# A counting sort's step on VectorE: the late count read in the middle of the next step

## What is computed

```python
x = _layernorm(x + _L0_gnn_ref(x, src, dst, edge_type_8, ...))          # gated recurrent update
x = _layernorm(x + _L1_gnn_ref(x, edge_attr_16, We, be, bias, src, dst, 12500))
x = _layernorm(x + _L2_gnn_ref(x, W1, root1, b1, W2, root2, b2, edge_index, edge_type_8))
x = _layernorm(x + _L3_gnn_ref(x, edge_index, W1, b1, W2, b2))
```

## Time and profile before

| | |
|---|---|
| median of 3 runs | 16680.38 us (16605.38 to 16702.47) |
| span of the profiled execution, first to last instruction | 16996.1 us |
| PE busy | 11995.3 us (71%) |
| DVE busy | 10824.2 us (64%) |
| ACT busy | 8088.7 us (48%) |
| POOL busy | 5158.9 us (30%) |
| mean granted TensorE clock | 0.791 |

### The profile page before, as it was taken

The page is one execution under the profiler, slowest core; times in us unless marked ns, Lnnn a source line. Parts: engine busy times, 40 slices in busy tenths (PEclk is TensorE's granted clock), DMA queues, the critical chain, the costliest instruction groups (busy, mean ns, idle before and its releaser), DMA issues. The chain is left out here.

```text
span 16996.1 us, 429738 instructions
## 1 busy us (share of the span) xinstructions
PE 11995.3 (71%) x146289; PEld 8312.1 (49%) x146290; DVE 10824.2 (64%) x19718; ACT 8088.7 (48%) x16130; POOL 5158.9 (30%) x4771
## 2 busy tenths in 40 slices
PE   1343443434434344799799998997996999999998
PEld 0111111111111111466688886665664888888887
DVE  3233333333333333688788887887886899999998
ACT  1232433433424234566466664665664555555554
POOL 1656666565664656000111111000000111111111
PEclk8555555555555555899899998999998999999999
DMA  7122222222222222688222222887885222333322
GB/s 208 48 72 59 81 67 66 81 59 71 74 58 79 58 72 82 184 229 229 89 106 106 106 106 95 234 235 198 235 235 126 80 83 83 85 85 84 84 84 71
DMA packets 1721891, 1905.31 MB, mean 112 GB/s; under 512 B 981549, under 2 KB 1429103, under 8 KB 1696207
## 3 DMA queue, kind: packets, MB, share of 16 engines
q1 hardware_dynamic: 1602775, 1863.79, 37.0%
q0 software_dynamic: 116864, 39.75, 1.5%
q10 hardware_dynamic: 2078, 0.15, 0.0%
HBM read 1449.57 MB, written 453.42 MB: 112 GB/s over the span
## 5 line engine op out<-in xcount | busy, mean ns | idle before, releaser
L688 POOL DMA_INDIRECT rec<-sort_ring,sort_idx x3520 | 4042.6, 1148 | 2791.9 <-issue 1469.7
L1381 DVE TENSOR_TENSOR e_full<-e_feats,e_masks 128x3840 bf16<-128x3840 bf16 x1179 | 2523.7, 2154 | 350.5 <-ACT e_feats L1339 302.0
L1294 PE MATMUL e_acc<-e_full,e_sel 128*128 128x384 bf16 (+1 forms) x11760 | 2120.9, 327 | 270.4 <-DVE e_full L1381 270.2
L778 PE MATMUL sort_ps_count<-sort_hot,upper_b 128*128 x400 | 231.6, 579 | 2689.9 <-DVE sort_hot L903 2144.6
L1530 PE MATMUL e_acc<-e_outer,e_sel 128*128 128x272 f32 x7840 | 1896.8, 397 | 3.9 <-DVE e_outer L1625 3.9
L1337 ACT CAST e_masks<-e_kind 128x1280 bf16<-128x1280 fp8e4 x1179 | 1482.6, 1258 | 629.5 <-DVE e_full L1381 575.0
L731 ACT CAST sort_cols_t<-sort_ps_late 120x256 f16<-120x256 f32 x98 | 39.5, 403 | 3439.8 <-remote 2373.0
L1530 PEld LDWEIGHTS e_acc<-e_outer,e_sel 128*128 128x128 f32 x7840 | 1459.2, 190 | 281.2 <-issue 4.1
L953 DVE TENSOR_TENSOR sort_over<-sort_ps_late,sort_late_base 128x20 f32<-128x20 f32 x175 | 30.7, 176 | 2428.1 <-remote 2208.7
L1294 PEld LDWEIGHTS e_acc<-e_full,e_sel 128*128 128x128 fp8e4 x11760 | 1061.0, 97 | 933.2 <-issue 298.1
L751 ACT ACTIVATE sort_made<-sort_ps_count,sort_window_bias 128x1024 fp8e4<-128x1024 f32 (+1 forms) x1274 | 1378.7, 1156 | 71.9 <-remote 26.7
(11 more groups left out here) (463 smaller groups left out, 22855.8 us busy)
## 6 DMA issues: line engine op xcount, KB each, us to landing
e_hot<-stream SPq DMA_DIRECT2D x888, 480.0 KB, 3.8
stream<-sort_made SPq DMA_DIRECT2D x98, 2568.0 KB
e_sel<-stream SPq DMA_DIRECT2D x1176, 160.0 KB, 2.7
e_st<-stream SPq DMA_DIRECT2D x99, 1888.0 KB, 7.3
sheaf_gather<-stream SPq DMA_DIRECT2D x393, 384.0 KB, 3.1
e_hot<-stream SPq DMA_DIRECT2D x294, 448.0 KB, 3.5
tail<-sort_made SPq DMA_DIRECT2D x98, 660.0 KB
sheaf_by_dst<-tail SPq DMA_DIRECT2D x491, 128.0 KB, 3.0
```

The costliest lines, as they stand in the source:

```text
L688: nc.gpsimd.indirect_dma_start(out=rec[q], out_offset=bass.IndirectOffsetOnAxis(ap=idx[:, s, q, c:c + 1], axis=0), in_=ring[:, s, q, c, :] ...
L1294: last = mm(acc[h][:, 0:cols_all], now[:, n * P:(n + 1) * P], full[q & 1][:, n, :], start=j == 0, stop=j == NT - 1)
L1381: v.tensor_tensor(full[q & 1][:, :, 0:cols].rearrange("p j (t k f) -> p j t k f", t=TYPES, k=3), feats[q & 1][:, :, :, :].unsqueeze(2).to_ ...
```

## The change

The late part of step i (L953 to L964) moves from the end of `place(i)` into the next step: after `find(i + 2)` and the ranks of step i + 1 up to L940, ahead of L943, which makes the next `late`. It gets a semaphore of its own, `late_step`, so `step` now counts 11 links. On DVE the first step of a quad is written out ahead of the loop, without a late part, and the late part of the last step follows the loop. PE's first two counts and first late count are written out ahead of its loop, in the order that they had. Since the loop now starts at the second step, every quad is given at least two steps (`2.0 * C` and the memset of `need` to 2).

```diff
-                link(v.tensor_scalar(span_i[:, 2:3], span[:, 3:4], float(C - 1), float(C), ALU.add, ALU.max))
+                link(v.tensor_scalar(span_i[:, 2:3], span[:, 3:4], float(C - 1), 2.0 * C, ALU.add, ALU.max))
...
-                v.memset(need[:, :, :], 1.0)
+                v.memset(need[:, :, :], 2.0)
...
-        LINKS = 14
+        LINKS = 11
+        LATE_LINKS = 3
...
                     count(i0 + n)
-                    with pe.Fori(i0, i1) as i:
+                    count(i0 + n + 1)
+                    count_late(i0)
+                    with pe.Fori(i0 + 1, i1) as i:
                         count(i + n + 1)
                         count_late(i)
...
-                def place(i, n):
+                def place_late(i):
+                    dve.wait_ge(late_counted, i + 1)
+                    v.tensor_tensor(over[:, :, :], ps_late, late_base[:, :].unsqueeze(2).to_broadcast([P, Q, C]), ALU.add)\
+                        .then_inc(late_step, 1)
+                    dve.wait_ge(late_step, 1)
+                    v.tensor_tensor(over[:, :, :], over[:, :, :], slot[:, :, :], ALU.subtract).then_inc(late_step, 1)
+                    v.tensor_tensor(late_base[:, :], late_base[:, :], ps_late_total, ALU.add)
+                    dve.wait_ge(late_step, 2)
+                    v.tensor_tensor(over[:, :, :], over[:, :, :], late[:, :, :], ALU.mult).then_inc(late_step, 1)
+                    dve.wait_ge(late_step, LATE_LINKS)
+                    dve.wait_ge(scattered, i + 1)
+                    dve.sem_inc(late_step, -LATE_LINKS)
+                    v.tensor_tensor(idx[:, place_of(i), :, :].squeeze(1), whole[:, :, :], over[:, :, :], ALU.add).then_inc(idx_ready, 1)
+
+                def place(i, n, before_it):
...
+                    if before_it is not None:
+                        place_late(before_it)
                     need(n_rank)
                     v.tensor_scalar(late[:, :, :], rank[:, :, :], float(P), None, ALU.is_ge).then_inc(late_made, 1)
...
-                    dve.wait_ge(late_counted, i + 1)
-                    n_over = made_one(v.tensor_tensor(over[:, :, :], ps_late,
-                                                      late_base[:, :].unsqueeze(2).to_broadcast([P, Q, C]), ALU.add))
...
                     find(i0, n)
-                    with dve.Fori(i0, i1) as i:
+                    find(i0 + 1, n)
+                    place(i0, n, None)
+                    with dve.Fori(i0 + 1, i1) as i:
                         find(i + 1, n)
-                        place(i, n)
+                        place(i, n, i - 1)
+                    place_late(i1 - 1)
                     dve.sem_inc(taken, 1)
```

More of the change, by code:

```diff
@@ L528, in sort_pass @@
         row_banks += [ps_count[:, a, :, :].rearrange("p w (k n) -> p (w k) n", n=P) for a in range(2)]
-        (keys_ready, fields_ready, idx_ready, scattered, hot_made, counted, taken, late_made, late_counted, step,
+        (keys_ready, fields_ready, idx_ready, scattered, hot_made, counted, taken, late_made, late_counted, step, late_step,
          rows_ready, rows_taken, codes_made, built, passed, sp_passed, base_made, ring_made, spill_made,
@@ L535, in sort_pass @@
                 "keys_ready", "fields_ready", "idx_ready", "scattered", "hot_made", "counted", "taken", "late_made",
-                "late_counted", "step", "rows_ready", "rows_taken", "codes_made", "built", "passed", "sp_passed",
+                "late_counted", "step", "late_step", "rows_ready", "rows_taken", "codes_made", "built", "passed", "sp_passed",
                 "base_made", "ring_made", "spill_made", "dve_passed", "pe_passed",
@@ L951, in place @@
                     n_whole = made_one(v.tensor_tensor(whole[:, :, :], part[:, :, :], trash[:, :, :], ALU.add))
-                    dve.wait_ge(late_counted, i + 1)
-                    n_over = made_one(v.tensor_tensor(over[:, :, :], ps_late,
-                                                      late_base[:, :].unsqueeze(2).to_broadcast([P, Q, C]), ALU.add))
[L955 to L960, removed]
                     need(n_whole)
-                    dve.wait_ge(scattered, i + 1)
                     dve.sem_inc(step, -LINKS)
-                    v.tensor_tensor(idx[:, place_of(i), :, :].squeeze(1), whole[:, :, :], over[:, :, :], ALU.add)\
-                        .then_inc(idx_ready, 1)
                     assert done[0] == LINKS, done
```

## The result

| kernel | median us | runs |
|---|---|---|
| before | 16691.43 | 4 |
| after | 17473.61 (17441.87 to 17485.22) | 4 |

The ratio is 1.0486 (1.0457 to 1.0515): slower by 782 us. The forecast was 16570 with a range to 16830; the way it went is rival C, though the time lies beyond the 17040 that C allowed.

What follows compares the result with a forecast made beforehand. Sort steps were taken to run on waits for a PE stalled while POOL scatters, no engine being full. Gain 115 us less 5 us for semaphores gave -110 us from the 16680.38 median: 16570 us, range for all cases 16400 to 16830.

Steps and rivals of the forecast that it cites:

- rival C: Sort: POOL may get a fifth step before falling silent, losing a quick step; slower, up to 17040 us; chance 0.22.
- The bound and the pattern: Sort steps: DVE waits at L953 for PE, 2208.7 us in 109 pieces; indices come quickly once POOL is silent.
- the delay of the first index: Start of a quad: first index waits for the next step's find and ranks, 5.5 us later, bounds 0 and 6.2.
- I expect all quads of this kind: 248.9 + 5.5 = 254.4: Sort: every quad has POOL silent after its fourth step; gain 4.8 us per quad, 24 x 4.8 = 115 us.
- the quad at 2343: Profiled quad before the change: POOL had four steps, resumed 116.8 us after its first scatter; period 248.9 us.
- some 10 us short: Fifth index at 116.8 us after a 9.6 us silence, against the 107 us within which POOL needs it.
- one more semaphore decrement per step: DVE: late_step's wait counts only in a quad's two unwaited steps, 0.1 to 0.26 us each; 5 us, at most 13.
- Peeled code: Written-out first steps, once per quad: no new engine work, 0 to 1 us per quad, 0 taken.
- The base of C's total: Sort: 274.2 us per quad set against the profile's mean of 259.2; 24 x 15.0 = 360 us more.
- A's sub-case: Sort stalls belong to the recording: POOL never starves, change touches nothing, timed kernel near 15770 us; within a 0.28 chance.
- predicted gain of 3.1 us per stalled step: PE in the sort: it no longer idles from L953 to the next L778; bounds 3.1 us and 0 per stalled step.

Runs made afterwards that it cites:

- hold_six: Kernel before, with the six first indices of a quad reported to POOL together; 16781.49 us, ratio 1.0110.
- after_again: Kernel after, no edit, run once more on chip D; 15938.86 us, ratio 1.0109.
- pad_65: Kernel before, with 65 matmuls of zeros into the histogram, once, ahead of the sort; 15774.54 us, ratio 1.0011 on chip D.
- cap_four: Kernel after, with the last three indices of a quad reported to POOL together; 16885.54 us, ratio 1.0175 to the kernel before on chip B.
- slow_step_three: Kernel before, with L959 three more times in a chain, about 0.6 us more per step; 17604.17 us, ratio 1.0581 on chip E.
- b_again: Kernel before, no edit, for a second profile on chip B; 16586.58 us (one execution).
- pe_peel: Kernel before, with only PE's first counts written out and at least two steps per quad; 17143.21 us, ratio 1.0102 on chip C.
- after_pe_loop_three: Kernel after, with PE's loop as before; 17237.29 us, ratio 1.0353 to the kernel before on chip E.

## Why the prediction was wrong

- **The bound and the pattern** were read rightly: steps wait on a PE that is slow while POOL scatters (hold_six), and periods hang on when POOL runs dry. So was the delay of the first index: 5.5 us forecast; on chip D it stands 46.2 us behind the memset in after_again and 40.9 in pad_65 (means of the quads), 5.3 later. One share is off without touching the sum: L953's 2208.7 us are 34% of 25 quads of 259.2 us, not 29%.
- **"I expect all quads of this kind: 248.9 + 5.5 = 254.4" is the step that failed.** It put the pause behind POOL's fourth step, as in the quad at 2343. The quads did become alike, but POOL got a fifth step: it is silent from 129 to 132 us and goes on at 137 to 144, where the forecast had 107 and 117. C named the condition, the fifth index within 107 us, and it was met at 98: three quick steps and a lead were more than the "some 10 us short". C gave it a chance of 0.22. cap_four, which takes the fifth step away and leaves the order and the form, brings the period back to 247.1 us, on chip B. That C's 274.2 us per quad lie so near the measured 271.8 is in part luck, since they start from a slower execution of before.
- **The term for one more semaphore decrement per step, "50 x 0.1 = 5 us, at most 13", was too small as well.** The rows show 0.16 us more before L922 and 0.42 more before L906 in an unwaited step, about 0.6 us together. What it costs hangs on the race with POOL: slow_step_three loses 934 us for it in the old order, while cap_four, with the same longer steps in the new order, stays within 2.5 us a quad of b_again. I had costed a delay by its own length in a loop whose length is set by a race. How much of the kernel after's loss it makes is not shown.
- **Peeled code, "0 taken"**, fits the sort as far as pe_peel shows. But PE's written-out code costs the last pass 180 to 202 us, though the diff touches nothing there, and the sum has no such term: 187 us in all on chip D.
- **The base of C's total** was off: 24 x 15.0 = 360 us was reckoned from a profile with 259.2 us per quad, while b_again, near the median, has 244.6. From there C is 24 x (274.2 - 244.6) = 710 us; after_pe_loop_three lost 567 us without a longer last pass, and the result 782 with it. A range around a median needs the period of a run at that median.
- **A's sub-case** said that without a stall the kernel would take 15770 us and the change would touch nothing. Chip D is that case: 15753 us, and 0.9996 with PE's loop as before. The prediction left the recording at most a quarter of the stall, since the median spoke against more; whether there is a stall at all depends on the chip. Beside it I had set the rule of the Trainium skill ("NOTIFIC — the notification-queue block", section 7.1) that the block which writes trace records pushes back when its inner queues fill. Chip D's executions were recorded as well and show no stall, so recording alone does not make it; that it takes part on the other chips no run here excludes.
- The predicted gain of 3.1 us per stalled step cannot be seen in the rows; the divided wait (L912 and L941) stands there instead.

What stays open: why PE is slow while POOL scatters, and why on some chips only. Instruction fetch is unlikely: b_again has 127 instruction packets between 300 and 6500 us, but none between 2264 and 2434, which spans a quad's stalled steps; the kernel after has one between 2421 and 2550, for stalled steps of 35.4 and 49.0 us. The Trainium skill ("Runtime: NRT & Kernel Launch", section "Instruction fetch mechanics") says that an engine's sequencer fetches its pages of instructions through a DMA queue of its own and that a taken branch out of the pages held forces a fetch. The trace of after_again's last pass has no instruction packet from 11912 to 15884 us, so no such fetch explains the dips of the clock. The new order without its 0.6 us was not tried.

## What to carry to other kernels

Where a loop races another engine and slows once that engine is fed, price an edit by which step it lets the other engine reach, not by its own microseconds: one step more before POOL ran dry cost about 25 us a quad (271.8 against 247.1), and 0.6 us a step cost 934 us in the old order. Measure a base on the same chip, and on more than one, before a gain of a per cent is believed. Writing out a first iteration is not free even off the path, as the last pass shows: look at the clock and length of every later pass.

## What was not expected of the hardware

- One of four chips ran the same program 839 to 1247 us faster, without the stall (periods of 205 to 206 us for kernels with the order of before, against 245 to 259).
- A step can take up to 49 us while POOL scatters (b_again) and takes 7.0 while it is silent (hold_six), though the DMA engines' share in the steps is only 0.14.
- Instructions put in ahead of a pass, and run once, changed its time by 178 us (4062 to 3884), with 285 us at clock 0.50 instead of 679, in stretches of 6.8 and 20.5 us.
